# The last group's router, its routing steps and its weights at later places in a transformer layer's schedule

## The reference

```python
x = layernorm(x + attention(x))                       # 16 heads, softmax, Wo
shared = (silu(x @ sw1) * (x @ sw3)) @ sw2            # 128 -> 256 -> 128
s = sigmoid(x @ router_w.T)                           # 8 scores for each token
top2 = top_k(s + router_bias, 2)
gates = s[top2] / sum(s[top2])                        # 1/2 each if the sum is not over 1e-9
comb = gates scattered to the 8 experts, 0 elsewhere
routed = sum over e of comb[:, e] * (gelu(x @ ew1[e]) @ ew2[e])
out = layernorm(x + shared + routed)
```

## Time and profile before

| | |
|---|---|
| median of 3 runs | 264.71 us (264.62 to 265.08) |
| the profiled execution: time, span | 265.03 us, 263.3 us |
| mean granted clock of TensorE | 0.934 |
| TensorE busy | 226.5 us, 86% |
| VectorE busy | 169.8 us, 64% |
| ScalarE busy | 137.3 us, 52% |
| GpSimd busy | 93.1 us, 35% |
| chain that ended last | PE 73%, DMA 7%, DVE 7%, POOL 5%, issue 4%, ACT 2% |

### The profile page before, as it was taken

The page is one execution under the profiler, slowest core; times in us unless marked ns, Lnnn a source line. Parts: engine busy times, 40 slices in busy tenths (PEclk is TensorE's granted clock), DMA queues, the critical chain, the costliest instruction groups (busy, mean ns, idle before and its releaser), DMA issues.

```text
span 263.3 us, 4349 instructions
## 1 busy us (share of the span) xinstructions
PE 226.5 (86%) x1514; PEld 153.9 (58%) x1514; DVE 169.8 (64%) x353; ACT 137.3 (52%) x262; POOL 93.1 (35%) x174
## 2 busy tenths in 40 slices
PE   1766964999999999993999999998866999999990
PEld 1434844767677676772677766565753566666640
DVE  8944991777969879794379761348354245665545
ACT  2452602677676667663266688866861243424230
POOL 8677480000101018031347956426187002020202
PEclk9998985899999999998599999999979799999996
DMA  7268856305538182466000000087700250100102
GB/s 179 65 91 92 85 69 99 35 11 87 44 54 76 27 81 28 82 47 227 2 0 7 0 7 2 4 316 324 319 2 0 80 243 0 34 8 0 40 6 75
DMA packets 12629, 19.42 MB, mean 74 GB/s; under 512 B 1296, under 2 KB 11728, under 8 KB 11952
## 3 DMA queue, kind: packets, MB, share of 16 engines
q1 hardware_dynamic: 12176, 18.49, 33.1%
q0 software_dynamic: 144, 0.39, 1.0%
q10 hardware_dynamic: 288, 0.27, 0.7%
HBM read 11.22 MB, written 1.11 MB: 47 GB/s over the span
## 4 chain that ended last, share of the span: by engine, by line
PE 73%; DMA 7%; DVE 7%; POOL 5%; issue 4%; ACT 2%; SPq 1%; POOLq 0%; DVEq 0%
PE ring L824 17%; PE pv_bank L838 14%; PE max_bank L810 11%; PE max_bank L948 10%; DMA qstack<-top_rows 5%; DVE kstack L632 3%; DMA kstack<-qk_parts 2%; PE ring L796 2%; PE ring L795 2%; PE ring L794 2%; PE max_bank L796 2%; PE max_bank L794 2%; PE max_bank L795 2%; PE misc_bank L877 1%; PE misc_bank L888 1%
## 5 line engine op out<-in xcount | busy, mean ns | idle before, releaser
L672 DVE TENSOR_REDUCE top<-max_bank 128x2 f32<-128x512 f32 x128 | 83.8, 683 | 33.1 <-PE max_bank L810 31.9
L571 ACT ACTIVATE probs_mem<-ring 128x512 f32<-128x512 f32 x128 | 73.9, 597 | 44.4 <-PE ring L824 43.1
L824 PE MATMUL ring<-qstack,kstack 128*128 128x256 f32 x256 | 62.7, 330 | 9.4 <-DMA qstack<-top_rows 9.4
L824 PEld LDWEIGHTS ring<-qstack,kstack 128*128 128x128 f32 x256 | 40.5, 199 | 37.2 <-ACT probs_mem L571 24.7
L810 PE MATMUL max_bank<-kstack,qstack 128*128 128x256 f32 x256 | 55.2, 305 | 3.8 <-DMA kstack<-qk_parts 3.2
L810 PEld LDWEIGHTS max_bank<-kstack,qstack 128*128 128x128 f32 x256 | 41.9, 203 | 8.0 <-DMA kstack<-qk_parts 4.0
L838 PE MATMUL pv_bank<-probs_mem,v 128*18 128x256 f32 x512 | 40.9, 393 | 0.0
L948 PE MATMUL max_bank<-probs_mem,wf 128*128 128x512 f32 x64 | 33.4, 608 | 0.0
L609 ACT ACTIVATE probs_mem<-ring 128x512 f32<-128x512 f32 x21 | 12.5, 597 | 20.8 <-PE ring L796 20.6
L794 PE MATMUL ring<-yt_hi,qk_parts 128*128 128x512 f32 x29 | 18.6, 640 | 3.0 <-DVE probs_mem L743 3.0
L477 POOL TENSOR_SCALAR rstd<-mv 128x2 f32<-128x2 f32 x8 | 1.8, 224 | 51.5 <-DVE mv L709 51.4
(11 more groups left out here) (143 smaller groups left out, 343.9 us busy)
## 6 DMA issues: line engine op xcount, KB each, us to landing
kstack<-gate_scratch SPq DMA_DIRECT2D x2, 2048.0 KB, 9.5
qstack<-gate_scratch SPq DMA_DIRECT2D x2, 2048.0 KB, 7.1
kstack<-qk_parts SPq DMA_DIRECT2D x24, 64.0 KB
wf<-w_ffn_dram SPq DMA_DIRECT2D x1, 1408.0 KB, 5.8
qstack<-qk_parts SPq DMA_DIRECT2D x9, 128.0 KB
xs<-x_dram SPq DMA_DIRECT2D x4, 256.0 KB, 5.1
kstack<-wf_hi SPq DMA_DIRECT2D x12, 64.0 KB
qstack<-wf_hi SPq DMA_DIRECT2D x6, 128.0 KB
```

The costliest lines, as they stand in the source:

```text
L571: nc.scalar.activation(probs[:, k // 2 % 4, c % 2 * 512:(c % 2 + 1) * 512], ring[k % NRING][:, :], ACT.Exp, scale=SCALE).then_inc(probs_ma ...
L672: dve.tensor_reduce(top[:, half, h:h + 3:2], max_bank[n % NMAX][:, :].rearrange("p (h k) -> p h k", h=2), AX.X, ALU.max).then_inc(max_take ...
L824: ins = mm(ring[k % NRING][:, j * S:(j + 1) * S], kstack[:, s, ab, r, kt * P:(kt + 1) * P], qstack[:, s, r, :], start=True, stop=True)
```

## The change

Four places in the table move, all of the last group. Its two routers go from tick 38 to tick 40, ahead of the first expert unit. Its routing steps are one step apart in ticks where they were in half ticks: `route0` at 41, `sig` 42, `route1` 43, `route2` 44, `route3` 46, `rank` 48, `route4` 49, `den` 50, `route5` 51. Its `combT` goes from tick 45 to 56 and its `load gates` from 46 to 57. On SyncE's queue the gates' load now stands behind the output store of group 0. No instruction's operands change, and the number of instructions stays the same except for ScalarE's table loads, which follow from the order of functions.

```diff
             late = b // 2 == NG - 1
-            router = 2 * (UP0 + 6) if late else 2 * first + (9 if b < 2 else 8)
+            router = 2 * EX0 if late else 2 * first + (9 if b < 2 else 8)
             jobs[router // 2, router % 2].append(("router", b))
             if b % 2:
 
                 for kind, n in (("route0", 1), ("sig", 2), ("route1", 3), ("route2", 4), ("route3", 6),
                                 ("rank", 8), ("route4", 9), ("den", 10), ("route5", 11)):
-                    n = router + n
+                    n = router + n * (2 if late else 1)
                     jobs[n // 2, n % 2].append((kind, b // 2))
 
-                comb_tick = {NG - 1: UP0 + 13, NG - 2: UP0 + 4}.get(b // 2, router // 2 + 7)
+                comb_tick = {NG - 1: EX0 + 16, NG - 2: UP0 + 4}.get(b // 2, router // 2 + 7)
                 for i in range(2):
                     jobs[comb_tick, i].append(("combT", b - 1 + i))
...
         for g in range(NG):
-            jobs[UP0 + (1, 2, 6, 14)[g], 1].append(("load gates", g))
+            jobs[(UP0 + 1, UP0 + 2, UP0 + 6, EX0 + 17)[g], 1].append(("load gates", g))
```

## The result

The changed kernel takes 257.13 us in the median of 4 runs (256.59 to 257.67), the kernel before 264.66 (263.18 to 265.08): ratio 0.9725, 95% interval 0.9682 to 0.9768. The prediction was 256.7 us with a range of 255.6 to 258.8. The profiled execution took 257.25 us with a span of 255.5, 7.8 less than the one of before; of these, 8.1 are made behind the last `yT` (the transposes of the last sequence's normalised values `y`, TensorE's row at 183.53 in the earlier trace rows) and 0.3 lost ahead of it.

What follows compares the result with a forecast made beforehand. TensorE was taken as the bound, heading the chain with 73%. Saving 8.7 us up to `down` 4, less 0.6 for `combT`, made 265.03 - 8.1 = 256.9, and 256.7 us as a median; range 255.6 to 258.8.

Steps and rivals of the forecast that it cites:

- The two waits: TensorE's waits near 190 (3.17 us, for hidden unit 7's product) and at `combT` (2.60 us, for `comb`) both disappear.
- The spacing: Last group's routing steps one tick apart instead of half a tick: no wait from them, value nothing.
- Hidden units 6 and 7 and the router: TensorE from 185.19: unit 6 to 186.59, a 0.15 us wait, unit 7 from 186.75 to 188.15, router to 189.40.
- ScalarE and `down` 0: First Gelu at 192.35, 0.45 us earlier; TensorE newly waits 0.8 us (0.3 to 1.3) before `down` 0, until 193.75.
- The sum: TensorE from 185.19 to `down` 4 needs 14.8 us instead of 23.5: 8.7 saved, less 0.6 for `combT`, 8.1.
- The clock: TensorE at full clock despite the new 0.8 us wait; the two dips behind the old waits, 3.3 us, go.
- rival A: TensorE's clock falls even so at the new wait ahead of `down` 0: 1.65 us more, 258.4 us; 10%.
- The noise: A measurement can tell about 0.2%, 0.5 us, from no change; faster 0.97, within it 0.01, slower 0.02.
- Rival B: ScalarE's table switch costs more than its row, up to another 1.28 us for each of two: 260.9 us; 3%.
- Rival C: Only one wait goes; a late `rank` or `den` holds up VectorE or TensorE elsewhere: about 261.0 us; 4%.
- Rival D: Last gates land late: TensorE held from a landing at 234.6 (slack 1.6 us), slower than before after 242.7; 1.5%.
- Rival E: The new wait at `down` 0 is absent: 256.0 us or a little under; 6%.

## Why the prediction was right, point by point

- **The two waits.** Both are gone, as forecast. What the prediction put down to the router's place (no Exp between Silu and Silu) was in good part `sig` ahead of the product: with the router back and only the steps apart, the wait falls from 3.01 to 1.57. Taking out two table loads at the old places shortens the same chain by as much. The prediction had `sig` in its account, but under the wrong part of the change.
- **The spacing.** "Value: nothing" was right of its cost (less the 0.29 by which this profile is late at the last `yT`: `rank` at 203.15 for 203.0 forecast, `den` at 206.25 for 206.2, `comb` at 209.20 for 210.9 at the latest) and left out what it brings. With the router at tick 40 the old spacing costs 2.2 us, a wait for `rank`; with the router at 38 the new spacing is what puts `sig` behind the product, and is worth 2.9 to 3.2. This is the step with a gap. Also missing in the account of before is that a wait for `rank` lies hidden behind the first dip, and comes up when TensorE gets there sooner.
- **Hidden units 6 and 7 and the router**: 0.15 forecast as a wait ahead of unit 7; from 186.65 + 0.23 = 186.88 to 187.06 it is 0.18. The routers start 0.12 later than forecast, at 188.56 - 0.29 = 188.27 for 188.15.
- **ScalarE and `down` 0**: first Gelu 192.75 - 0.29 = 192.46 for 192.35; `down` 0 193.83 for 193.75; new wait 194.12 - 193.39 = 0.73 for 0.8.
- **The sum**: `down` 4 comes 14.97 us after hidden unit 6 (200.45 - 185.48) for 14.8, so the difference is 8.54 and not 8.7. The forecast had no term for the first matmul behind a wait: hidden unit 7 takes 188.56 - 187.06 = 1.50 instead of 1.40, and `down` 0 to `down` 1 1.67 instead of 1.56. `combT` at tick 56 costs 0.44 (218.26 - 216.27 less a unit of 1.55) and not 0.60. 8.54 - 0.44 = 8.1.
- **The clock.** Full speed up to the last matmul, so rival A did not happen. The 3.3 us for the two dips were right for the profile on which the sum was made, 1.6 and 1.64 by the profiles without them; over executions they are not certain (77.8 beside 79.8 and 80.0), so against a kernel before without its second dip the gain is 6.1 and not 8.1. The medians give 7.5. That both dips stood in the one profile that the result was compared with is luck in a sum that came out at 8.1.
- **The noise.** The prediction took 0.2%, 0.5 us, as what can be told from no change; the 95% interval of the ratio is 0.4% to either side. The gain of 2.8% is far beyond both.
- **Rival B**, a dearer table switch: out, one load less saves 1.27. ScalarE: Activation LUTs, What ACT_TABLE_LOAD costs, in the Trainium skill gives 2.66 us in all for a switch; the traces here differ, and they decide. **Rival C** happened in the experiment with the steps half a tick apart, 1.79 of wait, and not in the changed kernel. **Rival D** has the right mechanism, with a slack of 2.9 us and not 1.6, because the six shared matmuls stand ahead of that `down`; the load landed 3.8 us ahead of its product.
- **Rival E**, no wait at `down` 0, took tanh to make: 0.8 us.

## What to carry to other kernels

When a side chain runs through two engines that also feed the main one, count how its steps stand in each engine's program order, not only how long it is: a step that waits for the other engine holds up the product behind it, and a little distance between the steps was worth more here than the router's new place. Before adding up what a removed wait gives, look for the wait that its lateness covers, by undoing one part at a time. And read a clock dip as a chance and not as a part of the wait: profile the same kernel more than once before its cost goes into a sum.

## What the runs showed of the hardware that was not expected

- The same wait of 3.0 us of TensorE was followed by a stretch at 1.2 GHz in three profiles and not in two; that of 2.5 to 2.6 in three and not in a fourth. When it came it cost 1.3 to 1.6 us, and 2.6 behind the wait of 3.87. Behind the wait of 3.01 the clock fell some 1.3 us after TensorE had gone on in two profiles of the kernel before, and ahead of that in the third, as with the gates at tick 64.
- A VectorE subtraction of two tensors in SBUF took 1.54 us instead of 0.69 while a GpSimd subtraction of the same kind (1.29 us, 179.40 to 180.69) ran. The Trainium skill, in SBUF — State Buffer, SBUF: two separate sides, says that a VectorE operation with two SBUF inputs and a GpSimd one that reads SBUF lock a shared port pair for the whole instruction, and the one that comes second blocks. By that rule, the trace agrees: an estimate of 180.69 - 179.71 = 0.98 us of block and 0.69 of work is 1.67 at the most, for 1.54 measured.
- Tanh behind Silu needed no table load of its own. In place of Exp it saved one load of 1.28 us between the last Silu and the first Gelu, and two where it stood between Silu and Silu.
